# Gated nodes: the slots' second normalisation on VectorE in place of ScalarE

## The reference

```
x = _layernorm(x + _L0_gnn_ref(...), axis=-1)     # two graph convolutions
x = _layernorm(x + _L1_gnn_ref(...), axis=-1)     # gated edges, batch norm
x = _layernorm(x + _L2_gnn_ref(...), axis=-1)     # attention, three heads
x = _layernorm(x + _L3_gnn_ref(...), axis=-1)     # six convolutions and a head
```

```
agg = (agg - mu_b) * jax.lax.rsqrt(var_b + EPS) * bn_gamma + bn_beta
h = agg + x
mu = h.mean(axis=-1, keepdims=True)
var = h.var(axis=-1, keepdims=True)
h = (h - mu) * jax.lax.rsqrt(var + EPS) * ln_gamma + ln_beta
h = jax.nn.relu(h)
return h + x
```

## Time and profile before

| | us |
|---|---|
| median of 3 runs (lowest to highest) | 10134.71 (10133.33 to 10137.58) |
| the profiled execution | 10122.26 |
| its span, from the first to the last instruction | 10120.5 |
| busy in the span: POOL, DVE, PE, ACT | 7733.6, 7342.6, 6368.1, 5860.5 |

### The profile page before, as it was taken

One profiled execution on the slowest core, in us unless ns is written; L12 is line 12 of the kernel. 1 busy time (PEld: TensorE's weight loads), 2 busy tenths in 40 slices (PEclk: granted clock), 3 DMA queues, 4 the chain that ended last, 5 costly groups with the idle time before them and its releaser, 6 DMA issues. The chain is left out here.

```text
span 10120.5 us, 131299 instructions
## 1 busy us (share of the span) xinstructions
PE 6368.1 (63%) x32436; PEld 5200.2 (51%) x32436; DVE 7342.6 (73%) x22503; ACT 5860.5 (58%) x13869; POOL 7733.6 (76%) x7194
## 2 busy tenths in 40 slices
PE   6027766667775566677856676786457676654444
PEld 3026655556554566677755666674234454432222
DVE  8359989956666877779988888665558776874444
ACT  0016677767776999989967888442125443432222
POOL 7756688877776988868847787677777777777777
PEclk8569988887887555578867888665558765765555
DMA  3999888842222777744424555464346443432222
GB/s 106 329 304 314 305 296 310 311 142 75 75 75 80 245 241 241 240 135 159 160 99 158 187 186 182 152 179 122 95 109 189 146 122 103 145 115 67 66 67 62
DMA packets 1019415, 1693.78 MB, mean 167 GB/s; under 512 B 304877, under 2 KB 535080, under 8 KB 1018594
## 3 DMA queue, kind: packets, MB, share of 16 engines
q1 hardware_dynamic: 782752, 1361.06, 39.1%
q0 software_dynamic: 175936, 218.82, 9.6%
q10 hardware_dynamic: 59970, 105.49, 3.0%
HBM read 988.03 MB, written 707.78 MB: 168 GB/s over the span
## 5 line engine op out<-in xcount | busy, mean ns | idle before, releaser
L1352 POOL DMA_INDIRECT g_got<-scaled,row_src x2352 | 2228.2, 947 | 788.0 <-issue 664.9
L904 DVE SCALAR_TENSOR_TENSOR g_sums<-g_got,first,g_sums 128x128 f32<-128x128 f32 (+3 forms) x3136 | 875.5, 279 | 1145.4 <-DMA g_got<-scaled,row_src 1135.4
L299 PE MATMUL g_a_p_z<-sb_L_gnn_W,g_a_u_t 128*128 128x128 f32 (+3 forms) x2574 | 578.5, 360 | 559.1 <-ACT g_a_u_t L1185 185.8
L908 DVE SCALAR_TENSOR_TENSOR g_sums<-g_sums,cont,g_got 128x128 f32<-128x128 f32 (+3 forms) x3128 | 882.6, 282 | 0.0
L1185 ACT COPY g_a_u_t<-g_a_p_t 128x512 f32<-128x512 f32 (+3 forms) x495 | 225.1, 455 | 1110.6 <-PE g_a_p_t L1137 648.9
L299 PE MATMUL g_bb_p_z<-sb_L_gnn_W,g_bb_u_t 128*128 128x128 f32 (+2 forms) x4302 | 749.9, 334 | 121.2 <-DVE g_bb_z L1079 60.9
L299 PEld LDWEIGHTS g_a_p_z<-sb_L_gnn_W,g_a_u_t 128*128 128x128 f32 (+1 forms) x2574 | 423.9, 235 | 727.0 <-ACT g_a_u_t L1185 402.7
L299 PEld LDWEIGHTS g_bb_p_z<-sb_L_gnn_W,g_bb_u_t 128*128 128x128 f32 x4302 | 659.8, 232 | 180.2 <-issue 150.7
L1185 ACT COPY g_bb_u_t<-g_bb_p_t 128x1024 f32<-128x1024 f32 (+2 forms) x294 | 233.9, 796 | 845.2 <-PE g_bb_p_t L290 842.2
L2464 POOL DMA_INDIRECT gb_got<-x,row_src x392 | 411.9, 1051 | 228.0 <-POOLq L178 123.9
L459 POOL DMA_INDIRECT f_got<-in_x,idx_dst x396 | 461.3, 1165 | 138.8 <-issue 120.1
(11 more groups left out here) (490 smaller groups left out, 23331.1 us busy)
## 6 DMA issues: line engine op xcount, KB each, us to landing
raw<-gb_u SPq DMA_DIRECT2D x98, 768.0 KB, 3.9
xs<-f_o ACTq DMA_DIRECT2D x97, 516.0 KB
f_x<-in_x ACTq DMA_DIRECT2D x97, 512.0 KB
g_bb_own<-in_x SPq DMA_DIRECT2D x97, 512.0 KB
wide<-g_bb_o SPq DMA_DIRECT2D x97, 512.0 KB
g_bb_own<-wide SPq DMA_DIRECT2D x97, 512.0 KB
g_bb_res<-in_x SPq DMA_DIRECT2D x97, 512.0 KB
x<-g_bb_o SPq DMA_DIRECT2D x97, 512.0 KB
```

Source lines behind the costliest of these rows:

```text
L299: last = nc.tensor.matmul(dst_psum[0:p, q * g * width:(q * g + n) * width], turned_tile[0:n * k, q * P:q * P + p], weight[0:n * k, 0:n * w ...
L904: nc.vector.scalar_tensor_tensor(out=self.firsts, in0=new, scalar=first[:, col], in1=self.firsts, op0=ALU.mult, op1=ALU.add).then_inc(run_ ...
L908: nc.vector.scalar_tensor_tensor(out=self.part(b.s, c), in0=before, scalar=cont[:, col], in1=new, op0=ALU.mult, op1=ALU.add).then_inc(run_ ...
L1352: pool.indirect_dma_start(got[b.s4][:, c * row:(c + 1) * row], None, table, bass.IndirectOffsetOnAxis(ap=index[:, b.n * CH + c:b.n * CH + ...
```

## The change

A new function of `GatedNode` issues, for a block of a, four tensor_scalar instructions on VectorE: o = y * rstd + nmr, with rstd and nmr read by pointer, a value to a partition. It has the waits of `normalise_2` and raises the same semaphore. In VectorE's list it stands with lag 6 between `stats_2` and `factors_1`; in ScalarE's list `na.normalise_2` is gone. The rows of b are normalised on ScalarE as before.

```
--- before
+++ after
@@ -1894,6 +1894,22 @@
                         act.wait_ge(m.turned, b.n - 1)
                     self.n2.scale(self.o_s[b.s], self.y_s[b.n % 4], b, self.first, p, j).then_inc(m.normed_b, 1)
 
+                def normalise_2_there(self, b):
+
+                    p, j = self.r.pj(b)
+                    m, dve = self.m, nc.vector
+                    dve.wait_ge(self.n2.factored, b.n + 1)
+                    if b.after(2):
+                        dve.wait_ge(m.stored[b.s], b.pair * DMA)
+                        dve.wait_ge(m.turned, b.n - 1)
+                    y, o = self.y_s[b.n % 4], self.o_s[b.s]
+                    for q in range(j):
+                        i = self.first + q
+                        last = nc.vector.tensor_scalar(o[0:p, q * D:(q + 1) * D], y[0:p, q * D:(q + 1) * D],
+                                                       self.n2.rstd[b.s][0:p, i:i + 1], self.n2.nmr[b.s][0:p, i:i + 1],
+                                                       ALU.mult, ALU.add)
+                    last.then_inc(m.normed_b, 1)
+
                 def evacuate(self, b):
                     p, j = self.r.pj(b)
                     m, act = self.m, nc.scalar
@@ -1994,13 +2010,13 @@
 
                         pipeline(dve, [(na.scores, 9, NBA), (nb.scores, 9, NB), (stats_1, 2, NBA), (factors_2, 6, NBA),
                                        (na.shift, 5, NBA), (nb.shift, 5, NB), (na.rectify, 5, NBA), (nb.rectify, 5, NB),
-                                       (stats_2, 5, NBA), (factors_1, 2, NBA)])
+                                       (stats_2, 5, NBA), (na.normalise_2_there, 6, NBA), (factors_1, 2, NBA)])
 
                     @block.scalar
                     def _(act):
                         act.wait_ge(prepared, 5)
                         pipeline(act, [(n2.root, 6, NBA), (na.normalise_1, 3, NBA), (nb.normalise_1, 3, NB), (n1.root, 2, NBA),
-                                       (na.normalise_2, 6, NBA), (nb.normalise_2, 6, NB), (na.evacuate, 7, NBA),
+                                       (nb.normalise_2, 6, NB), (na.evacuate, 7, NBA),
                                        (nb.evacuate, 7, NB)])
 
                     @block.tensor
```

## The result

| | us |
|---|---|
| before, median of 4 runs (lowest to highest) | 10136.15 (10133.33 to 10139.06) |
| after, median of 4 runs (lowest to highest) | 10406.21 (10404.45 to 10422.12) |
| after / before, 95% interval | 1.027 (1.0252 to 1.0288) |
| profiled execution of after, its span | 10404.45, 10402.7 |

The change costs 270 us: slower, as forecast, and 84 us less than the forecast of 10490.

What follows compares the result with a forecast made beforehand. The prediction took ScalarE alone to bound the gated nodes' 11.02 us turn; blocking on GpSimd would make it 14.8, 94 x 3.78 = +355 us, giving 10490. Own range 10440 to 10560; 8-in-10 range 10065 to 10560.

Steps and rivals of the forecast that it cites:

- What bounds the kernel, and the relief: Gated nodes pass: ScalarE alone sets the 11.02 us turn; the move takes 1.54 us off it; GpSimd's 9.83 is next.
- The collision: Gated nodes pass: the four new one-input SBUF to SBUF VectorE instructions and GpSimd block each other; turn 14.8 us.
- One by one or all through one opening: Whether an opening in GpSimd's work admits one waiting VectorE instruction (forecast, chance 0.58) or all four (0.24).
- third rival: Only one or two of the four wait, for a single product each: 11.5 to 13 us a turn, 10185 to 10335; chance 0.09.
- the forecast's own bounds: Turn of the one-by-one case: 14.3 us (instructions of 0.13, sequence starting half a microsecond earlier) to 15.4 us.
- first rival: One opening lets all four through; GpSimd loses 0.6 to 0.8 us a turn and bounds at 10.5: 10084 us; chance 0.24.
- The second: Rival: VectorE and GpSimd don't block each other; GpSimd's 9.83 us bounds: 10018 us, or VectorE's 9.99: 10033; chance 0.09.
- Where a seam has no opening: In GpSimd's gapless third cn_a_v, cn_b_v, a blocked VectorE instruction waits to the end, about E + 14.0.
- The size: Turn of 14.8 us, 3.78 more than 11.02, in 94 turns: +355 us.
- The price of one: One new tensor_scalar on VectorE: 0.19 us undisturbed, from above 0.26; four take 0.86 us.
- Moved waits: Waits for factored, stored and turned, now on VectorE, and readers of cn_a_o one turn behind: no cost counted.
- What would show it: Profile after: tensor_scalar mean above 1 us, singles of 1.3 and 3.6, ScalarE idle 4 to 5 a turn, turn 14.8.

Runs made afterwards that it cites:

- one: Changed kernel with one of the four rows normalised on VectorE and three on ScalarE, a semaphore for each part: 10090.97 us, 0.9967 of the kernel before.
- two: Changed kernel with two of the four rows normalised on VectorE and two on ScalarE: 10067.25 us, 0.9943 of the kernel before.
- psum3: As `psum4`, but three rows on VectorE and the fourth back on ScalarE: 10027.99 us, 0.9893 of the kernel before.
- psum4: Changed kernel with the four instructions as scalar_tensor_tensor, second operand from PSUM, written by one more instruction: 10035.12 us, 0.9903 of the kernel before.
- mid: Changed kernel with the four instructions directly behind factors_2 instead of behind stats_2: 10148.5 us, 1.0024 of the kernel before.
- both: ScalarE normalises all rows as before; VectorE repeats the four into an unread tile, without waits for store and turn: 10406.86 us, 1.0281 of the kernel before.
- twoin: As `psum4`, but with the second operand left in SBUF: 10417.16 us, 1.028 of the kernel before.
- split: Changed kernel with GpSimd's product for cn_b_v in two halves of 4 rows, no wait between: 10294.73 us, 1.0176 of the kernel before.

## Why the prediction was right in sign and too large

- *What bounds the kernel, and the relief.* Right. ScalarE alone set the turn, and 1.54 us a turn was its part: `one` and `two` give it back in quarters, and `psum3` and `psum4` come with 9.88 and 9.92 us (the median turn of `psum4`) close to the 9.83 that GpSimd's work needs.
- *The collision.* Right: the new instructions block on GpSimd, and with the second operand in PSUM they don't.
- *One by one or all through one opening.* Right, one at each. But none waited through two products, as the forecast had it for the third: the second, third and fourth wait for a single product each (1.28, 1.26 and 2.34 us). The turn of 13.92 us lies in the gap between the third rival (11.5 to 13) and the forecast's own bounds (14.3 to 15.4). That the time is inside the wide range is owed to the range's reach down to the first rival, and it is 6 us above the 10400 that the prediction named as its own sign of being wrong. The first rival (10084) is refuted by the single instructions of 1.30, 1.42 and 2.38 us. The second (10018 to 10033) would have been right only without the blocking; `psum4`, at 10035, is that case.
- *Where a seam has no opening.* Wrong. The prediction said that a blocked instruction "isn't let in at the seams of a sequence without gaps, only after it", from the one gb_a_n_nmr. The third went in between the third cn_a_v and cn_b_v. This cost little, since the fourth had to wait for cn_b_v in any case: it is most of term (3) of the next point. The trace of the kernel before already held the contrary case, with two inputs in SBUF, in another pass (the second line merges two instructions):

```profile
5197.18 0.63 DVE L346 SCALAR_TENSOR_TENSOR ga_b_n_nmr<-ga_b_n_stats,ga_b_n_rstd 128x8 f32<-128x8 f32 x1
...
5195.16 4.40 POOL L2121 TENSOR_TENSOR ga_b_x_beta<-ga_b_x,row_L_gnn_ln_b 128x1024 f32<-128x1024 f32 x2
```

  The first of the two lasts 2.63 us, to 5197.79, and the second begins at 5197.75. The VectorE instruction ends at 5197.81, with the first, and does not wait for the second, which ends at 5199.56.
- *The size.* 3.78 us a turn was forecast, 2.90 came; 0.88 is too much, in three terms, from E (3833.52, the end of factors_1). (1) ScalarE gave cn_b_y to GpSimd at E + 4.84, not 5.1, as its eight instructions ended in 3.17 us in place of 3.46: 0.26. (One begins every 0.385 us in both kernels, but the last one's record is 0.48 us long, where before the change the median of cn_b_y's is 0.76.) (2) From there to the end of cn_b_v the prediction had 14.0 - 5.1 = 8.9 us, and the trace has 8.58. The starts of the earlier trace rows give 8.61 (3844.00 to 3852.61); "about 10.2" and "about 14.0" were rounded up at each step: 0.32. (3) From the end of cn_b_v to the end of factors_1 it had 0.8, and 0.50 were taken (3846.94 to 3847.44), as only one instruction was left, and it ended 0.09 behind cn_b_v: 0.30. Together 0.88, and times 94 that is 83 of the 84 us of the error. Beside this the upper end of the forecast's own range doesn't follow from its 15.4 us: 10134.71 + 94 x 4.38 is 10546, not 10560.
- *The price of one.* 0.19 us was taken, from the copy from SBUF to SBUF, and 0.26 was the upper bound. The upper bound was right (`mid`), and for the turn it made no difference.
- *Moved waits.* Right, nothing (`both`).
- *What would show it.* A mean above 1 us, ScalarE idle for 4 to 5 us a turn ahead of cn_a_y, and GpSimd busy for about 130 of 200 us came (4.32, 139.16). Single instructions of 3.6 us did not, for the reason of the fourth point, nor did a turn of 14.8 us.

Open: why gb_a_n_nmr was held over four GpSimd instructions before. `twoin` excludes that it is the two inputs in SBUF and `split` that it is a missing wait, for the instructions of this pass. Nor is it the rule for gb_a_n_nmr itself. In the trace of the kernel before, 70 of its 198 last over 0.3 us, and 68 of these end with the first product that stands in their way. Only the first two were held past a seam, for 3.47 and, at 5369.17, for 2.19 us, and it is the first two in the trace of every other kernel here as well (3.23 to 3.50 and 2.18 to 2.20 us). In `two` one that began at 5581.42, during a gb_own_w that ended at 5581.95, ended at 5581.97, though gb_a_x_beta had followed at 5581.91. What is special about the first two turns of that pass no run shows.

## What to carry to other kernels

Before work goes to VectorE beside a busy GpSimd, count the new instructions whose inputs and output all lie in SBUF. Here each of them that did not meet an opening waited for the end of the GpSimd instruction that was running, so N short ones cost up to N of GpSimd's durations, however little they do themselves. What took back a part of the loss here, or all of it and more: one operand from PSUM, one wide instruction in place of the N, shorter GpSimd instructions, a place where GpSimd is idle, or no more of them than the engine's slack can take. An engine's busy share doesn't show such a wait, but the spread of one shape's durations (318 to 2380 ns) does, and so does an instruction count that falls while the busy time rises.

## What the runs showed of the hardware

- In this pass a waiting VectorE instruction was let in at the end of the GpSimd product in its way, also where the next one began at once: all 281 long ones of the kernel after ended 0.08 to 0.09 us behind such an end, and all 281 of the two-input form of `twoin` 0.15 us behind it. One that began just before a seam missed it and waited for the next product: once in the kernel after (0.06 us before the seam), 18 times in `mid` (0.02 to 0.08). In another pass two instructions, the first two gb_a_n_nmr, were held longer (3.47 and 2.19 us), unexplained.
- The narrow ones hardly slowed GpSimd down: its products keep 2.34 to 2.35 and 1.26 to 1.28 us, the figures of the earlier trace rows; in `twoin` cn_b_v takes 2.39. The one of 512 columns cost it 0.19 us (1.46 for 1.27).
- tensor_scalar from SBUF to SBUF of 128 columns was no faster undisturbed (0.26 us each, `mid`) than the form with an operand in PSUM ((0.84 - 0.34)/2 = 0.25 us in `psum3`). Beside GpSimd its median was 1304 ns where that form's was 339.
